# First graph layer: the gather program of GpSimd without loops, waiting for three of each four gathers to land

## The reference

```python
src, dst = edge_index[0], edge_index[1]
Qh, Kh, Vh = (x @ Wq.T + bq), (x @ Wk.T + bk), (x @ Wv.T + bv)     # each reshaped to (n, 4, 16)
Ee = (edge_attr @ We.T + be).reshape(-1, H, D)
score = (Kh[src] * Qh[dst] * (1.0 / np.sqrt(D)) * Ee).sum(-1)
score = jnp.exp(jnp.clip(score, -5.0, 5.0))
msg = Vh[src] * score[..., None]
wV = jax.ops.segment_sum(msg, dst, num_segments=n)
x = _layernorm(x + wV)
```

## Time and profile before

| | us |
|---|---|
| median of 3 runs | 2007.81 |
| lowest and highest | 1999.49, 2012.04 |
| the profiled execution, whole | 2009.44 |
| its span | 2007.7 |
| the gathers of the first layer, from the first issue to the end of the last | 58.30 to 1069.10 |

### The profile page before, as it was taken

One profiled execution on the slowest core, in us unless ns is written; L12 is line 12 of the kernel. 1 busy time (PEld: TensorE's weight loads), 2 busy tenths in 40 slices (PEclk: granted clock), 3 DMA queues, 4 the chain that ended last, 5 costly groups with the idle time before them and its releaser, 6 DMA issues. The chain is left out here.

```text
span 2007.7 us, 45198 instructions
## 1 busy us (share of the span) xinstructions
PE 1441.3 (72%) x13291; PEld 1224.7 (61%) x13291; DVE 1357.2 (68%) x3516; ACT 1031.9 (51%) x2313; POOL 1285.1 (64%) x1384
## 2 busy tenths in 40 slices
PE   5477777767676676767665885684798888788884
PEld 4355555555555555555554885474687777777873
DVE  5777777777777777777777787887656554554443
ACT  2444444444444444444443950594276676666560
POOL 1577777777777777777772850263576676666661
PEclk7688888888888878888886897697778888888776
DMA  5333333333333333333322200003322222222111
GB/s 84 101 81 82 81 81 82 81 81 81 81 81 78 79 82 81 81 81 81 81 74 67 73 35 4 1 2 111 58 58 47 57 48 48 51 55 48 37 27 22
DMA packets 126435, 128.43 MB, mean 64 GB/s; under 512 B 81779, under 2 KB 89127, under 8 KB 126044
## 3 DMA queue, kind: packets, MB, share of 16 engines
q0 software_dynamic: 37824, 64.91, 15.9%
q1 hardware_dynamic: 62934, 54.96, 9.0%
q10 hardware_dynamic: 25542, 6.81, 1.5%
HBM read 116.63 MB, written 9.93 MB: 63 GB/s over the span
## 5 line engine op out<-in xcount | busy, mean ns | idle before, releaser
L634 POOL DMA_INDIRECT shared<-kv_tab,idx x784 | 766.1, 977 | 296.8 <-issue 238.3
L837 PE MATMUL bank<-key_hot,lo_hot 128*128 128x350 f16 x784 | 182.7, 337 | 291.9 <-DVE count L698 240.1
L2271 POOL DMA_INDIRECT count<-att_tab,count x302 | 290.3, 961 | 157.6 <-issue 69.2
L837 PEld LDWEIGHTS bank<-key_hot,lo_hot 128*128 128x128 f16 x784 | 55.7, 97 | 379.6 <-issue 365.7
L698 DVE TENSOR_TENSOR count<-count,bank 128x350 f32 x392 | 205.3, 524 | 82.2 <-issue 39.9
L770 ACT ACTIVATE lo_dist<-iota_neg,tile_lo 128x128 f16<-128x128 f32 x784 | 238.5, 389 | 0.0
L683 DVE TENSOR_SCALAR key_hot<-iota_key,tile_key 128x350 f16<-128x350 f16 x784 | 196.0, 321 | 0.0
L2631 ACT ACTIVATE shared<-shared 128x128 f32<-128x128 bf16 x384 | 161.4, 483 | 29.4 <-PE bank L2776 23.1
L704 DVE TENSOR_TENSOR prod<-bank,shared 128x512 f32<-128x512 f32 x98 | 67.8, 692 | 148.4 <-DMA shared<-kv_tab,idx 145.7
L852 PE MATMUL bank<-hots,msg 128*65 128x64 f32 x1568 | 164.6, 285 | 0.0
L852 PEld LDWEIGHTS bank<-hots,msg 128*65 128x65 f32 x1568 | 163.8, 200 | 0.4 <-DVE msg L725 0.4
(11 more groups left out here) (523 smaller groups left out, 2990.2 us busy)
## 6 DMA issues: line engine op xcount, KB each, us to landing
shared<-in_edge_attr SPq DMA_DIRECT2D x97, 256.0 KB, 3.0
shared<-kv_tab,idx POOLq DMA_INDIRECT x784
shared<-lo_tab SPq DMA_DIRECT2D x24, 512.0 KB, 3.8
count<-att_tab,count POOLq DMA_INDIRECT x302, 2.5
qwin<-q_tab ACTq DMA_DIRECT2D x196, 16.0 KB
kv_tab<-count SPq DMA_DIRECT2D x1, 1600.0 KB, 10.4
idx<-in_src SPq DMA_DIRECT2D x97, 4.0 KB, 1.6
g_edge<-att_tab,count POOLq DMA_INDIRECT x96, 2.5
```

The lines of the kernel that those rows point to most:

```text
L634: nc.gpsimd.indirect_dma_start(kv[:, s, c, :], None, kv_tab, bass.IndirectOffsetOnAxis(ap=idx[:, s, c:c + 1], axis=0)).then_inc(kv_in[s], 16)
L837: last = nc.tensor.matmul(bank[6 + q % 2][:, 0:KC], lo_hot[:, c, :], key_hot[:, c, :], start=i == 0, stop=i == GT - 1)
L2271: nc.gpsimd.indirect_dma_start(ring[s][:, j, 0:D + 2], None, att_tab[1], bass.IndirectOffsetOnAxis(ap=src_i[:, t:t + 1], axis=0)).then_inc ...
```

## The change

POOL's program is written out for all 98 groups. The marks `half_done` of DVE are gone, with both of POOL's waits for them. Behind the gathers c = 3 and c = 7 of each group POOL waits until the first three of these four, and all earlier ones of that slot, have landed; the fourth is counted on a semaphore of its own. The wait for the indices of the next group stands behind c = 4. Thresholds are constants plus a term of j. DVE waits for both semaphores of the slot, and 8 counts are subtracted at the end instead of 4.

```diff
-        ea_in, kv_in = [short_sem(f"a_ea{s}") for s in range(RS)], [short_sem(f"a_kv{s}") for s in range(RS)]
+        ea_in = [short_sem(f"a_ea{s}") for s in range(RS)]
+        kv_first, kv_last = ([short_sem(f"a_kv_{of}{s}") for s in range(RS)] for of in ("first", "last"))
...
+        STREAK = 4
+        KV_LAST = 16 * C // STREAK
+        KV_FIRST = 16 * C - KV_LAST
...
                 with pool.Fori(0, nj) as j:
-                    def gather(g, s, m):
-
-                        pool.wait_ge(half_done, (j * G + g) * 2 + 1)
+                    def indices(g):
+
+                        s = g % RS
+                        pool.wait_ge(idx_in[s], j * (uses(s) * 16) + (g // RS + 1) * 16)
                         pass_on(pool)
-                        pool.wait_ge(idx_in[s], (j * uses(s) + m) * 16)
-                        pass_on(pool)
+
+                    indices(0)
+                    for g in range(G):
+                        s, m = g % RS, g // RS + 1
                         for c in range(C):
-                            if c == C // 2:
-
-                                pool.wait_ge(half_done, (j * G + g) * 2 + 2)
-                                pass_on(pool)
                             nc.gpsimd.indirect_dma_start(
                                 kv[:, s, c, :], None, kv_tab, bass.IndirectOffsetOnAxis(ap=idx[:, s, c:c + 1], axis=0)
-                            ).then_inc(kv_in[s], 16)
-
-                    each(pool, gather)
-                    forget_rows(pool, kv_in, slot_free, cleared, (j + 1) * G + RS)
+                            ).then_inc((kv_last if c % STREAK == STREAK - 1 else kv_first)[s], 16)
+                            if c == C // 2 and g + 1 < G:
+                                indices(g + 1)
+                            if c % STREAK == STREAK - 1:
+
+                                pool.wait_ge(kv_first[s], m * KV_FIRST - 16 * (C - 1 - c) * (STREAK - 1) // STREAK)
+                    pool.wait_ge(slot_free, (j + 1) * G + RS)
+                    pass_on(pool)
+                    for s in range(RS):
+                        nc.gpsimd.inc_swdge_sem([kv_first[s]], [uses(s) * KV_FIRST], mode="sub")
+                        nc.gpsimd.inc_swdge_sem([kv_last[s]], [uses(s) * KV_LAST], mode="sub")
+                    pool.sem_inc(cleared, 1)
...
                 dve.sem_inc(slot_free, RS)
-                dve.sem_inc(half_done, 3)
...
-                        dve.wait_ge(kv_in[s], m * (16 * C))
+                        dve.wait_ge(kv_first[s], m * KV_FIRST)
+                        dve.wait_ge(kv_last[s], m * KV_LAST)
...
-                        nc.vector.tensor_tensor(prod[:, :], prod[:, :], bank[4][:, :], ALU.mult).then_inc(half_done, 1)
+                        nc.vector.tensor_tensor(prod[:, :], prod[:, :], bank[4][:, :], ALU.mult)
...
-                        dve.sem_inc(half_done, 1)
```

More of the change, by code:

```diff
@@ L590, in build @@
         count_clear = short_sem("a_count_cleared")
-        half_done = short_sem("a_half_done")
-        loop_sems = [begun, slot_free, *idx_in, *ea_in, hot_ok, ea_t, ea_ts, hot_t, hot_ts, ee_ok, qd_ok, sc_ok, ex_ok, msg_ok, sum_ok,
-                     cleared, q_in, key_ok, lo_ok, count_ok, bank_free, count_clear, half_done]
+        STREAK = 4
+        KV_LAST = 16 * C // STREAK
+        KV_FIRST = 16 * C - KV_LAST
+        loop_sems = [begun, slot_free, *idx_in, *ea_in, *kv_first, *kv_last, hot_ok, ea_t, ea_ts, hot_t, hot_ts, ee_ok, qd_ok, sc_ok, ex_ok, msg_ok, sum_ok,
+                     cleared, q_in, key_ok, lo_ok, count_ok, bank_free, count_clear]
         nc.clear_and_free_semaphores(early_sems)
```

## The result

| | before | with the change |
|---|---|---|
| median, us | 2006.69 (4 runs) | 2039.24 (4 runs, 2031.74 to 2047.36) |
| ratio | | 1.0171, 95% interval 1.0123 to 1.0219 |
| span of the profiled execution | 2007.7 | 2036.3 |
| stretch of the gathers of the first layer | 58.30 to 1069.10 = 1010.8 | 51.01 to 1089.89 = 1038.9 |

The kernel is 1.7% slower. The forecast was 2053 with a range of 2032 to 2090.

The account below looks back on a forecast made before the run. POOL's gather cadence in the first layer was taken as the bound. Waits +51, stall -6.1 and end +0.5 sum to +45.4 us, 2054.8 against the profiled 2009.4; as a median 2053, range 2032 to 2090.

Parts of the forecast that it names:

- The bound: First layer: POOL's gather cadence sets the period, and each us added to its sequence moves the layer's end by one.
- up to 1.5 us a group downward: First layer: time taken from POOL's sequence shortens the layer, up to DVE's 1.5 us a group of waiting for gathers.
- The stall at the start: First layer's start: POOL's one 6.4 us wait for DVE's L712 goes with the marks, gaining 6.1 us.
- The new waits: POOL's waits behind c = 3 and c = 7: 195 with an excess of 0.26 us each, +51 us.
- The choice between the readings: Price of POOL's new waits: three readings gave 36, 46 and 85 us; 0.26 each was taken, a little above the typical pause.
- the first reading: Low price of the new waits, with POOL released as DVE is, 2.72 us after issue: 195 x 0.185 = 36 us.
- The step from 0.235 to 0.26: New waits: the later layer's typical excess of 0.235 us raised because a gather carries 64 KB against 33 KB there.
- The gathers' own duration: POOL's gathers in the first layer: mean duration still near 977 ns with the change.
- the pause takes the conflict away: Rival, first layer: pauses bring back 25 us of gathers lengthened beside DVE's work; +20, 2028 us; chance 0.09.
- Loops, registers, DVE's marks: POOL's written-out program and DVE's changed mark and waits: no gain or loss, 0.
- The end: After the last L736: four more subtractions cost between 0 and 1.3 us, 0.5 taken.
- met waits: Rival, POOL's new waits: three gathers have always landed when POOL looks, every pause stays 0.305; 2002 us; chance 0.06.

Follow-up runs that it names:

- The last pair of runs: hots_early and before_hots_early: the same DVE reordering on the changed kernel without waits and marks (1.0025), and on the kernel before (1.0011).
- both_first_waits_2: Changed kernel with its waits, DVE's hots moved ahead of the first addition of counts and msg ahead of the second; 1.0224 against the kernel before.
- before_hots_early: Kernel before, loop and marks kept, with DVE's hots put behind its second product and msg behind the first addition of counts; 1.0011.
- both_first_2: Changed kernel without its waits, DVE's hots moved ahead of the first addition of counts and msg ahead of the second; 0.9948 against the kernel before.
- hots_early: Changed kernel without waits and marks, DVE's hots put behind its second product and msg behind the first addition of counts; 1.0025 against the kernel before.
- all_four: Changed kernel with each new wait also for the fourth gather; stretch of the gathers 1398.5 us, on the chip with 2716.76 us for the kernel before.

## Why the prediction was right, and where it was off

The direction, the mechanism and the range held; the shift was +45 us in the forecast and +32.5 between the medians.

*The bound.* POOL set the pace of the layer, and each us in its sequence moved the end: stretch +28.1 us, span +28.6. Right. The supplement, "up to 1.5 us a group downward", was wrong, and nothing of the forecast rested on it; it is the kernel before that shows a nearer bound. The 1.5 us was DVE's wait for gathers, but the row of PE that DVE needs as well, L814, ended only some 0.8 us before DVE's start (516.62 + 0.53 against 517.98 in the timeline). The last pair of runs met that ring.

*The stall at the start*, -6.1: measured, no wait for a mark is left. Right.

*The new waits*, 195 x 0.26 = 51: measured 194 x 0.252 = 48.8. The choice between the readings, near the typical pause of the like waits elsewhere and not their mean, was right, and so, as far as the traces show, was its reason: pauses of 1 us were rare (3 of 194, the longest 1.2), and SP's load is issued at 509.37, behind the third gather of the second half (506.60). That a met wait costs nothing is shown by the wait for the first two of four. That the whole price is lateness of the landing, as I first thought, is not so: of the 0.25 us nearly all is the 0.259 from landing to POOL's start, which the first reading had in it unseen, as DVE's 2.72 us from issue to start. The step from 0.235 to 0.26 for a gather of 64 KB instead of 33 came out at 0.252, but by luck: the landing is 2.5 us here and 2.5 there, so no row shows that the size made a difference.

*The gathers' own duration*, forecast unchanged at 977 ns: measured 958 ns, -15.0 us. This is the failed step, the overlap of POOL's gathers with DVE's work, put at no change. The mean fell 19 of the 32 ns towards 945, which the prediction itself had named as a sign of being wrong, and its 15 us are about the gap between +45 and +32.5; the total stayed inside the range, near its lower end. I had it as a rival, "the pause takes the conflict away", with a chance of 0.09 and 25 us, and argued against it that DVE and POOL start from the same landing and shift together. They do not: c = 0 begins 1.61 us behind the issue of c = 7 and not 1.32, and c = 4 begins 4.02 us behind DVE's first product (504.10 - 500.08) and not 3.57 (511.38 - 507.81), because each pause adds its excess to all gathers behind it while DVE's chain runs on from the landing of c = 7. That was enough to carry the beginnings of c = 4 and c = 5 past `hots` and `msg`. What stayed is c = 7, inside the 2 us of `key_hot`, so 15 of the 25 came back. That the cause is the beginnings and not the waits as such is shown by `both_first_waits_2`, which has the waits and long gathers (987 ns), and by `before_hots_early`, which has neither the waits nor long gathers (956 ns). The excess was in front of me by gather: the 25 us lie on c = 4, 5 and 7, and the timeline shows which of DVE's instructions runs when each begins.

*Loops, registers, DVE's marks*, 0: right, by the kernel with only the loop written out. *The end*, +0.5: measured +1.0, inside its bounds of 0 to 1.3, twice what I took.

Of the rivals, met waits did not happen: the estimate from the Trainium skill's page (DMA: Bandwidth & Descriptors, "Anatomy of one DMA — SWDGE (gpsimd) path"), 2.15 us for 64 KB, would have made the waits free. The trace disagrees: the gathers waited for land 2.52 us after their issue, against 2.195 for the fourth one's end. By this landing alone the waits would have cost 0.02 us or less; the 0.259 us from landing to start decided.

The section "Mode Summary", from which the prediction takes that DVE's second port is shared with GpSimd, stands in the Trainium skill on the page Advanced Engine Details and Errata, not on the one that the prediction names. It says that GpSimd instructions and DVE's two-port instructions interfere or block each other. The durations agree in so far as the gathers that begin within a product of two SBUF tiles are longer, and show no such effect for a gather already under way beside one (504.10 in the changed kernel). That the port is what the gathers wait for is not shown by any run here; the runs show only when they are longer, and by how much.

## What to carry to other kernels

A wait that was met early costs nothing, and one whose event comes just in time can still cost the time from event to start (0.26 us here). So ask when the waiting engine would be released, not only when the transfer has landed, and move the condition one transfer earlier, as with two of four instead of three, before taking it away. Where one engine sets the pace, a pause in it also shifts it against the others; look at which of its instructions are longer than their minimum, what runs beside their beginnings, and where the pause will put them. And before promising a gain below the pace-setter, follow every input of the engine that waits for it, not only the one named as releaser: here the second bound was 0.8 us away, or nothing at all once DVE's order was changed.

The fastest kernel of this study, both_first_2, is 0.5% under the kernel before (0.9948, 0.9917 to 0.9979). Its gathers account for 5 us of stretch, about half of that; hots_early, with the same stretch of 1005.6 us on another chip, came out at 1.0025, so the other half is not to be relied on. The change as it stands gains 6.1 us by dropping the marks and pays 48.8 for its waits, of which 15 come back.

## What the runs showed of the hardware

- A gather of GpSimd that begins while DVE works on a product of two f32 SBUF tiles (0.69 us) is longer by what is left of that product less 0.128 us (875 gathers in ten profiles, to within 0.01 us). One that begins in the product's first 0.045 us, or was begun before it, is not longer. Inside `key_hot` (eight short DVE instructions on f16, 1.9 to 2.0 us) a gather is longer by 0.00 to 0.10 us if it begins in the first 0.6 us of the row, and behind that by 0.07 to 0.09 in nearly all of 911 cases, whatever is left.
- A gather waited for has landed 2.52 us after its issue. POOL, waiting for the third of four, starts the next gather 0.259 us after the landing event, 2.78 us after the issue. With a wait for the fourth as well it starts 0.737 us after the event, 3.26 us after the issue (`all_four`). A wait met 0.9 us or more before adds nothing to the usual pause of 0.305 us (783 pauses with the wait for the first two).
- One chip ran the kernel before in 2716.76 us instead of 2005. The profiles of the variants from it have idle times of up to 7.5 us on DVE for which the trace names no engine of this core, and a mean granted clock of 0.73 instead of 0.81. On it the kernel with the waits and the new DVE order was 1.6% faster than before in three of four executions, where on an ordinary chip it was 2.2% slower. A difference of a per cent or two on one chip need not hold on the next.
